# Two-layer graph network: both halves of eight weight chunks made inside the edge loop, one-hots for two edge tiles at once, biases by TensorE, second node half first

## The reference

```python
# layer 0
feat  = concat([x[src], x[dst]], axis=1)              # 8192 x 2048
e_f   = relu(feat @ W_kind + b_kind)                  # kind hh: 128 edges, oo: 640, ho: 7424
logit = e_f @ W_a + b_a
alpha = softmax of logit over the edges of one target
z     = segment_sum(alpha * x[src], dst)              # 256 x 1024
new   = relu(concat([x, z], 1) @ W_hn + b_hn)         # nodes 0 to 63
        relu(concat([x, z], 1) @ W_on + b_on)         # nodes 64 to 255
x1    = layernorm(x + new)
# layer 1
h  = x1 @ W
e  = exp(-leaky_relu((h @ a_l)[src] + (h @ a_r)[dst]))
hp = segment_sum(e * h[dst], src) / (rowsum + eps)
out = layernorm(x1 + elu(hp))
```

## Time and profile before

| | us |
|---|---|
| median of 3 runs | 383.04 (382.99 to 384.62) |
| the profiled execution | 383.35 |
| its span, first to last instruction | 381.3 |
| mean granted clock of TensorE | 0.934 of 2.4 GHz |
| TensorE (matmul) busy | 326.5 |
| VectorE busy | 301.9 |
| ScalarE busy | 189.9 |
| GpSimd busy | 136.8 |

### The profile page before, as it was taken

One profiled execution on the slowest core, in us unless ns is written; L12 is line 12 of the kernel. 1 busy time (PEld: TensorE's weight loads), 2 busy tenths in 40 slices (PEclk: granted clock), 3 DMA queues, 4 the chain that ended last, 5 costly groups with the idle time before them and its releaser, 6 DMA issues.

```text
span 381.3 us, 4671 instructions
## 1 busy us (share of the span) xinstructions
PE 326.5 (86%) x1434; PEld 252.7 (66%) x1434; DVE 301.9 (79%) x400; ACT 189.9 (50%) x289; POOL 136.8 (36%) x202
## 2 busy tenths in 40 slices
PE   2899999999999998999999999638899962898570
PEld 1678877776547866888888887426688841686320
DVE  0799999959799687999999997985677789436445
ACT  3745594220333349788787764250566581251143
POOL 3200070370008002988988773910024231016000
PEclk9999999999999999999999999885999995699685
DMA  7997698899989960002003003333638960000002
GB/s 232 412 400 292 238 345 298 278 244 275 354 297 377 388 243 2 0 3 112 0 2 111 3 3 89 131 110 119 211 106 332 306 250 2 0 2 1 0 0 110
DMA packets 17639, 63.63 MB, mean 167 GB/s; under 512 B 2234, under 2 KB 2236, under 8 KB 17360
## 3 DMA queue, kind: packets, MB, share of 16 engines
q1 hardware_dynamic: 13520, 50.34, 36.2%
q0 software_dynamic: 2096, 8.74, 7.8%
q10 hardware_dynamic: 2000, 4.26, 3.2%
HBM read 60.16 MB, written 3.16 MB: 166 GB/s over the span
## 4 chain that ended last, share of the span: by engine, by line
PE 64%; DVE 25%; DMA 4%; ACT 4%; issue 2%; SPq 0%; DVEq 0%; ACTq 0%
PE ps L1240 20%; PE ps L1067 10%; PE ps L1131 7%; DVE W_lo L669 6%; PE ps L1089 6%; PE ps L1247 3%; PE ps L1273 3%; PE ps L1106 3%; PE ps L1304 3%; PE ps L1336 3%; DMA W_raw<-in_L_gnn_W_dram 2%; PE ps L1281 2%; DMA x_nat<-in_x_dram 2%; DVE tile_val L690 1%; DVE small L957 1%
## 5 line engine op out<-in xcount | busy, mean ns | idle before, releaser
L432 ACT CAST W_hi<-W_raw 128x1024 fp32r<-128x1024 f32 x72 | 73.2, 1046 | 67.9 <-DMA W_raw<-in_L_gnn_W_ho_dram 24.6
L669 DVE TENSOR_TENSOR W_lo<-W_raw,W_hi 128x1024 fp32r<-128x1024 f32 x56 | 73.7, 1342 | 23.2 <-ACT W_hi L432 20.7
L905 DVE SCALAR_TENSOR_TENSOR ps<-ps,wa_bc 128x1024 f32<-128x1024 f32 x74 | 87.6, 1277 | 1.9 <-PE ps L1240 1.9
L364 POOL TENSOR_TENSOR W_lo<-W_raw,W_hi 128x1024 fp32r<-128x1024 f32 x16 | 39.4, 2468 | 82.0 <-ACT W_hi L432 82.0
L1240 PE MATMUL ps<-A_tab,oh 128*128 x148 | 53.5, 443 | 2.2 <-ACT oh L541 2.2
L390 POOL TENSOR_SCALAR sc_r<-irow,keys 128x64 f32<-128x64 f32 x74 | 35.0, 472 | 39.1 <-PE ps L1247 38.7
L1067 PE MATMUL ps<-W_hi,xT_hi 128*128 128x512 f32 x112 | 46.5, 415 | 0.9 <-DVE W_lo L669 0.9
L1240 PE MATMUL ps<-B_tab,oh 128*128 x148 | 46.4, 394 | 0.0
L1067 PE MATMUL ps<-W_lo,xT_hi 128*128 128x512 f32 x112 | 44.1, 394 | 0.0
L547 ACT ACTIVATE sc_l<-sc_l,keys 128x64 f32<-128x64 f32 x74 | 24.6, 341 | 21.8 <-DVE ps L905 15.5
L1067 PE MATMUL ps<-W_hi,xT_lo 128*128 128x512 f32 x112 | 34.5, 390 | 0.0
(11 more groups left out here) (229 smaller groups left out, 546.7 us busy)
## 6 DMA issues: line engine op xcount, KB each, us to landing
W_raw<-in_L_gnn_W_oo_dram SPq DMA_DIRECT2D x8, 1024.0 KB, 9.7
W_raw<-in_L_gnn_W_ho_dram SPq DMA_DIRECT2D x8, 1024.0 KB, 4.9
W_raw<-in_L_gnn_W_hh_dram SPq DMA_DIRECT2D x8, 1024.0 KB, 8.4
W_raw<-in_L_gnn_W_hn_dram SPq DMA_DIRECT2D x8, 1024.0 KB, 5.3
W_raw<-in_L_gnn_W_on_dram SPq DMA_DIRECT2D x8, 1024.0 KB, 6.0
W_raw<-in_L_gnn_W_dram SPq DMA_DIRECT2D x4, 1024.0 KB, 7.6
key_rows<-key_rows_scratch POOLq DMA_DIRECT2D x1, 2304.0 KB, 14.0
table_scratch<-tabs ACTq DMA_DIRECT2D x2, 1024.0 KB, 6.4
```

Source lines behind the costliest of these rows:

```text
L364: ga.tensor_tensor(W_lo[:, ring(n), :], W_raw[:, n // 2 % NS, n % 2, :], W_hi[:, ring(n), :].bitcast(F32), ALU.subtract).then_inc(lo_pool, 1)
L432: sa.copy(W_hi[:, ring(n), :], W_raw[:, n // 2 % NS, n % 2, :]).then_inc(hi_made, 1)
L669: v.tensor_tensor(W_lo[:, ring(n), :], W_raw[:, n // 2 % NS, n % 2, :], W_hi[:, ring(n), :].bitcast(F32), ALU.subtract).then_inc(lo_made, 1)
L905: v.scalar_tensor_tensor(acc, acc, 0.0, wa_bc[:], ALU.max, ALU.mult, accum_out=keys[:, t, 2:3]).then_inc(reduced, 1)
```

## The change

Six edits:

1. In the loop GpSimd makes the four one-hots of two tiles by two instructions over 256 elements (subtract, then compare with zero). They wait for the scatter of tile t-3. `sc_l` and `sc_r` become one buffer `sc`.
2. GpSimd makes the low halves of all eight chunks 48 to 55 in the loop (after tiles 8, 16, ..., 64), and ScalarE the eight high halves. Chunks 52 to 55 ("apart") have high halves in buffers of their own and low halves in place in `W_raw`. The transfers into these places wait until the chunks are used. From chunk 56 on GpSimd begins only after P.
3. The maximum of the static logits is taken ahead of the loop, so that behind it only the new part is reduced.
4. The biases `b_hn` and `b_on` are split into two parts and added by six matmuls of TensorE; VectorE's additions L976 and L982 go. ScalarE copies 64x2048 elements, VectorE subtracts 32x2048, GpSimd makes the pick matrix.
5. The update's order changes, so that the hn chunks end four chunks before the last; rows 0 to 63 are finished early.
6. The late half 1 of the nodes goes first through the layernorm and into layer 1. x1's half 0 is transposed between chunks 81 and 82 of half 1. The low halves of chunks 80 to 82 are made after the first part of half 0.

```diff
+        def apart(n):
+            return END["hoB"] + NB <= n < UX
+        def in_ring(n):
+            return [m for m in range(n + 1) if split(m) and not apart(m)]
+        def halves(n):
+            if apart(n):
+                return hi_apart[n - END["hoB"] - NB], lo_in_raw[:, n // 2 % NS, n % 2, :]
+            return W_hi[:, ring(n), :], W_lo[:, ring(n), :]
...
-        END = {"ooA": 8, "ooB": 16, "hoA": 30, "hh": 40, "hoB": 48, "updx": 64, "upd": 80, "h1": 88}
+        END = {"ooA": 8, "ooB": 16, "hoA": 30, "hh": 40, "hoB": 48, "hn": 76, "upd": 80, "h1": 88}
+        update_order = [("hn", 0), ("on", 0), ("hn", 2), ("on", 2), ("hn", 4), ("on", 4), ("hn", 6), ("hn", 8), ("on", 6),
+                        ("hn", 10), ("on", 8), ("hn", 12), ("on", 10), ("hn", 14), ("on", 12), ("on", 14)]
...
# SyncE
-                    if not split(last_of):
+                    if not split(last_of) or apart(last_of):
                         sp.wait_ge(chunk_used, last_of + 1)
...
# GpSimd, ends(t)
                 if t >= U:
-                    pool.wait_ge(scattered, 1 + JO + t - U + 1)
-                ga.tensor_scalar(sc_r[:, t % U, :], irow[:, 1:Q + 1], keys[:, t, 0:1], None, ALU.is_equal)
-                ga.tensor_scalar(sc_l[:, t % U, 1, :], irow[:, 1:Q + 1], keys[:, t, 1:2], None, ALU.is_equal) \
-                  .then_inc(ends_made, 1)
+                    pool.wait_ge(scattered, 1 + JO + t + 2 - U)
+                pair = sc[:, t % U:t % U + 2, 0:2, :]
+                link(ga.tensor_tensor(pair, irow[:, 1:Q + 1].unsqueeze(1).unsqueeze(1).broadcast_to([P, 2, 2, Q]),
+                                      keys[:, t:t + 2, 0:2].unsqueeze(3).broadcast_to([P, 2, 2, Q]), ALU.subtract))
+                ga.tensor_scalar(pair, pair, 0.0, None, ALU.is_equal).then_inc(ends_made, 1)
...
-            for t in range(NT):
+            for t in range(0, NT, 2):
                 ends(t)
-                if t % 12 == 8 and t // 12 < NB:
-                    lows(END["hoB"] + t // 12, END["hoB"] + t // 12 + 1)
-
-            lows(END["hoB"] + NB, len(chunks))
+                if t % 8 == 0 and 8 <= t <= 64:
+                    lows(END["hoB"] + t // 8 - 1, END["hoB"] + t // 8)
+
+            pool.wait_ge(gathered, NT)
+            link(ga.memset(pick_f[:], 0.0))
+            for r in (0, Q // 2):
+                link(ga.memset(pick_f[r:r + 1, 0:P], 1.0))
+            ga.nop().then_inc(pick_made, 1)
+            pool.wait_ge(dve_step, dve_at("P"))
+            lows(UX, len(chunks))
...
# ScalarE, in the loop
-                if j % 6 == 3 and j // 6 < NB:
-                    high(END["hoB"] + j // 6)
+                if j % 4 == 2 and END["hoB"] + j // 4 < UX:
+                    high(END["hoB"] + j // 4)
...
# ScalarE, behind the loop
-            highs(END["hoB"], END["hoB"] + NB)
+            act.wait_ge(pick_made, 1)
+            sa.copy(pick[:], pick_f[:])
+            act.wait_ge(biases_in, 112)
+            sa.copy(bn_parts[:], bn_rows).then_inc(act_step, 1)
+            high(UX)
+            high(UX + 1)
...
# VectorE
+            top = soft.rearrange("p (h n) -> p h n", h=2)
+            link(v.tensor_tensor(top, S_log[:, 0, :, :], S_log[:, 1, :, :], ALU.max))
+            link(v.tensor_reduce(small[:, 44:46], top, AX, ALU.max))
...
-            link(v.tensor_tensor(top_static[:], top_static[:], S_log[:, 2, :, :], ALU.max))
-            link(v.tensor_reduce(small[:, 2:4], top_static[:], AX, ALU.max))
+            link(v.tensor_reduce(small[:, 2:4], S_log[:, 2, :, :], AX, ALU.max))
+            link(v.tensor_tensor(small[:, 2:4], small[:, 2:4], small[:, 44:46], ALU.max))
...
             lows(UX, UX + NB)
+            dve.wait_ge(act_step, act_at("parts"))
+            link(v.tensor_tensor(bn_parts[Q // 2:Q], bn_rows[Q // 2:Q], bn_parts[Q // 2:Q].bitcast(F32), ALU.subtract))
+            stage("parts")
...
-            for q, acc in ((0, G0[:, D:2 * D]), (1, G1[:, 0:D])):
-                own = slice(q * Q, (q + 1) * Q)
-                dve.wait_ge(act_step, act_at(f"q{q}_low"))
-                link(v.tensor_tensor(y2[own, 0, :], y2[own, 0, :], bn_bc[own, 0, :], ALU.add))
-                link(v.tensor_tensor(y1[own, 0, :], y2[own, 0, :], acc[own, :], ALU.add))
-            link(v.scalar_tensor_tensor(y1[:, 0, :], y1[:, 0, :], 0.0, x_nat[:, 0, :], ALU.max, ALU.add))
+            dve.wait_ge(act_step, act_at("q0_low"))
+            link(v.tensor_tensor(G0[0:Q, D:2 * D], G0[0:Q, D:2 * D], y2[0:Q, 0, :], ALU.add))
+            link(v.scalar_tensor_tensor(y1[0:Q, 0, :], G0[0:Q, D:2 * D], 0.0, x_nat[0:Q, 0, :], ALU.max, ALU.add))
+            lows(END["upd"], END["upd"] + NB - 1)
+            dve.wait_ge(chunk_used, END["upd"])
+            link(v.scalar_tensor_tensor(y1[:, 1, :], G1[:, D:2 * D], 0.0, x_nat[:, 1, :], ALU.max, ALU.add))
+            statistics(1)
+            stage("var1")
+            dve.wait_ge(act_step, act_at("q1_low"))
+            link(v.tensor_tensor(G1[Q:P, 0:D], G1[Q:P, 0:D], y2[Q:P, 0, :], ALU.add))
+            normalise_second_half(x1[:, 1, :], "sd1")
+            stage("x1_1")
+            link(v.scalar_tensor_tensor(y1[Q:P, 0, :], G1[Q:P, 0:D], 0.0, x_nat[Q:P, 0, :], ALU.max, ALU.add))
             statistics(0)
             stage("var0")
...
+            x1_low(1)
+            first_half_scale("sd0")
+            stage("scale0")
+            lows(END["upd"] + NB - 1, END["upd"] + NB)
+            x1_low(0)
...
# TensorE, behind the second part of z
+                if s == 1:
+                    pe.wait_ge(dve_step, dve_at("parts"))
+                    for acc, k, columns in ((G0[:, D:2 * D], 0, slice(Q, Q + P)), (G1[:, 0:D], 1, slice(Q, Q + P)),
+                                            (G1[:, D:2 * D], 1, slice(0, P))):
+                        for f in range(0, D, 512):
+                            mm(acc[:, f:f + 512], pick[:, columns], bn_parts[:, k, f:f + 512], start=False, stop=False,
+                               skip_group_check=True)
...
+            transpose_x1(1)
             for g in range(END["upd"], END["h1"], NB):
-                block_by_block(g, G1, END["upd"], "x1T", "h_0" if g + NB == END["h1"] else None)
+                block_by_block(g, G1, END["upd"], "x1T", "h_1" if g + NB == END["h1"] else None, (1, 0),
+                               (lambda: transpose_x1(0)) if g == END["upd"] else None)
```

More of the change, by code:

```diff
@@ L429, in high @@
                 act.wait_ge(w_in[n // 2 % NS], 16 * (n // 2 // NS + 1))
-                if n >= NB:
-                    act.wait_ge(chunk_used, before_in_ring(n) + 1)
-                sa.copy(W_hi[:, ring(n), :], W_raw[:, n // 2 % NS, n % 2, :]).then_inc(hi_made, 1)
+                if len(in_ring(n)) > NB and not apart(n):
+                    act.wait_ge(chunk_used, in_ring(n)[-1 - NB] + 1)
+                sa.copy(halves(n)[0], W_raw[:, n // 2 % NS, n % 2, :]).then_inc(hi_made, 1)
             def highs(a, b):
@@ L580, in _ @@
                     .then_inc(act_step, 1)
[L581 removed]
+            high(UX + 2)
+            high(UX + 3)
             for s in range(2):
@@ L612, in normalise_first_half, with x1_high @@
                     .then_inc(act_step, 1)
+            def x1_high(h):
+                act.wait_ge(pe_step, pe_at(f"x1T{h}"))
+                sa.copy(xT_hi[:, :, h * P:(h + 1) * P], G0[:, h * D:(h + 1) * D].rearrange("p (c n) -> p c n", n=P)) \
+                    .then_inc(act_step, 1)
+            act.wait_ge(dve_step, dve_at("var1"))
+            deviation(1)
+            x1_high(1)
             act.wait_ge(dve_step, dve_at("var0"))
@@ L617, in _ @@
             normalise_first_half(x1[:, 0, :])
-            act.wait_ge(dve_step, dve_at("var1"))
-            deviation(1)
-            for h in range(2):
-                act.wait_ge(pe_step, pe_at(f"x1T{h}"))
-                sa.copy(xT_hi[:, :, h * P:(h + 1) * P], G0[:, h * D:(h + 1) * D].rearrange("p (c n) -> p c n", n=P)) \
-                    .then_inc(act_step, 1)
+            x1_high(0)
             highs(END["upd"], END["h1"])
             warm_up(ACT.Exp, 1)
-            for h in range(2):
+            for h in (1, 0):
                 act.wait_ge(dve_step, dve_at(f"dots{h}"))
@@ L668, in low @@
                     dve.wait_ge(hi_made, hi_count(n))
-                    v.tensor_tensor(W_lo[:, ring(n), :], W_raw[:, n // 2 % NS, n % 2, :],
-                                    W_hi[:, ring(n), :].bitcast(F32), ALU.subtract).then_inc(lo_made, 1)
+                    hi, lo = halves(n)
+                    v.tensor_tensor(lo, W_raw[:, n // 2 % NS, n % 2, :], hi.bitcast(F32), ALU.subtract).then_inc(lo_made, 1)
             def lows(a, b):
@@ L1056, in split_chunk @@
                 pe.wait_ge(lo_pool if by_pool(n) else lo_made, lo_count(n, by_pool(n)))
-                return W_hi[:, ring(n), :], W_lo[:, ring(n), :]
+                return halves(n)
             def dense(a, b, acc, hi, lo, blocks, first, end):
@@ L1075, in x_dense, with block_by_block @@
```

(12 more changed lines are left out.)

120 lines of the change are left out of this document (61 added, 59 removed).

## The result

| | before | after |
|---|---|---|
| median (lowest to highest) | 383.31 (382.99 to 384.62), 4 runs | 377.38 (376.57 to 378.31), 4 runs |
| profiled execution, its span | 383.35, 381.3 | 376.57, 374.5 |
| mean granted clock, of 2.4 GHz | 0.934 | 0.950 |

After over before is 0.984 (95% interval 0.981 to 0.987): 1.6% faster, 5.9 us at the medians. 372.0 was forecast and the range ended at 377.0. The kernel is faster, as said, but gives half of the gain; the time is just outside the range. The profiled execution was the fastest of the four, so the traces show 6.8 us of gain and the medians 5.9.

What follows compares the result with a forecast made beforehand. VectorE was taken to pace the loop and softmax, TensorE the update, VectorE's work the standstill before layer 1. Terms -8.2 - 0.9 + 1.4 - 7.3 + 1.5 + 2.5 = -11.0 from 383.35 gave 372.3, 372.0 as median; range 368 to 377.

Steps and rivals of the forecast that it cites:

- What bounds the kernel: Whole kernel: loop at VectorE's pace with TensorE close behind, softmax VectorE's, update TensorE's, then TensorE stands still before layer 1.
- 8.45 us transfer: Before layer 1: low halves of chunks 80 and 81 waited 8.45 us for a transfer, ahead of VectorE's node halves.
- Softmax: Behind the loop: without GpSimd beside them VectorE's operations run short and the merged maximum saves a pass; 8.2 us less.
- P to z: From P to z's low half: TensorE's clock stays up or falls late, VectorE's bias subtraction caps the gain; 0.9 less.
- Biases on TensorE: In the update: six added matmuls of 512 columns cost 1.4 us more.
- Tail: From the update's last matmul to layer 1: half 1 goes first, low halves 80 to 82 lie ahead; 7.3 us less.
- Layer 1: In layer 1: half 0's transposes between chunks 81 and 82 add 1.0 to 2.0 us, taken as 1.5.
- The loop: Edge loop: each of eight low halves between pairs holds TensorE by 0.7 us, of which 2.5 us more is left.
- the dearer loop: Edge loop: pair near 1.9 us or ScalarE late with eight high halves; +3 to +6, 375 to 378; chance 0.10.
- The slower case: Edge loop: GpSimd becomes the loop's engine through costly rows of 64; 385 at a pair of 2.5 us; chance 0.06.
- free loop: Edge loop costs nothing because the compare runs faster than the 2048-element row; 369.5 us (368 to 371); chance 0.26.
- The page on one-input operations: GpSimd in the loop: page says one-input operations run roughly at line-rate; pair near 1.3 us, loop would cost nothing.

Runs made afterwards that it cites:

- e7: Kernel before, with VectorE's low halves of chunks 80 and 81 moved from ahead of the first layernorm to behind x1; 385.3 us, 1.005 of before.
- e5: Changed kernel with GpSimd's low halves of chunks 52 to 55 behind the loop again, the other four in the loop; 378.1 us, 0.987 of before.
- e2: Changed kernel with end one-hots made for one tile at a time again, all eight low halves still in the loop; 370.8 us, 0.966 of before.
- e6: Kernel before with only the paired end one-hots, four buffers, four low halves in the loop; 385.9 us, 1.008 of before.
- e8: e1 plus 14 extra matmuls keeping TensorE busy until about P, and VectorE's bias subtraction moved behind z's first part; 369.1 us, 0.964 of before.
- e1: Changed kernel with six buffers for the end one-hots instead of four; 371.0 us, 0.967 of before.
- e9: e1 plus only the 14 extra matmuls on TensorE, results unused; 373.3 us, 0.973 of before.

## Why the prediction was wrong, step by step

- **What bounds the kernel: right**, except for the 8.45 us transfer, which I read as something the tail stood behind and which holds nothing (e7).
- **Softmax: right**, -8.2, with the four durations as forecast. e5 shows the price of contention depends on which instructions meet, which I needed only for before.
- **P to z: the size agrees, -1.1 for -0.9, but partly by luck.** The forecast had the clock stay up or fall late. It fell as before, and rose about 3.7 us behind the start of the first 16 matmuls in place of 6.0 (estimates from the windows of both traces). Kernels with the same code there took 8.8 to 9.3 (e2 to e5), and those with the old code 8.6 (e6) and 9.6 (e7), so a term of 1.1 is no larger than what this stretch varies by itself. That VectorE's bias parts cap the gain was right in kind: with both causes gone there are 2.3 more (e8).
- **Biases on TensorE: right.** The six matmuls take 1.58 us in the chain; forecast 1.4.

```profile
258.61 5.55 PE ps L1357 x16
...
267.25 3.72 PE ps L1357 x16
...
275.57 1.58 PE ps L1366 x6
```

- **Tail: right**, -6.8 for -7.3; it is 10.2 in every kernel with the change and 16.9 to 17.0 in the kernel before and e6. The low halves of chunks 80 to 82 end at 310.47, 0.4 behind TensorE's last matmul, which is most of what is missing; the prediction had named this risk. **Layer 1: +1.2 for +1.5**, also partly by luck: half 0's transposes take 0.87, below the 1.0 to 2.0 forecast, and the kernels with the old order take 23.5 (before), 24.0 (e7) and 24.6 (e6).
- **The loop: wrong, and it is the step that failed.** The mechanism was named (a pair, a low half and the next pair stand ahead of a scatter), but its price was not: +2.5 was forecast, +6.5 measured, and 96.0 is over the 92 that the prediction gave as a sign of being wrong. Its sum was 8 x 0.7 for the stalls, less 1.3 of head start, less 1.8 that TensorE regains. The stall itself was nearly right: I put 0.7, from 6.3 for GpSimd's path and 5.6 for TensorE's; measured are 5.95 (1.55 + 2.37 + 1.53 + 0.5) and 5.36, so about 0.58. A cheaper pair and a faster TensorE cancel. The term that failed is the one that I put at nothing: **TensorE pays 0.48 to restart behind a scatter that waited**, so a stall is 1.06 and eight are 8.5 for 5.6, 2.9 more. The other 1.1 is in what I took off. The head start was worth 0.7 and not 1.3 (at the first stall, 1.06, the spacing of VectorE's reductions grew by 0.35), and it is never rebuilt. The regain is 1.06 - 0.88 = 0.18 between two low halves, 1.3 over seven intervals and not 1.8 over the loop. So all seven later stalls came through: 7 x 0.88 + 0.3 = 6.5, the measured term. I also let the loop go free at a pair of 1.54. By that formula the measured pair of 1.53 would have cost nothing, and the kernel would have come to 369.5; the path of TensorE in it, 5.6 for 5.36, was too long.
- **Of the rivals** the dearer loop (375 to 378) is what happened, though by neither cause it named: the pair was not near 1.9 and ScalarE was not late (it waits 19.8 us for GpSimd). It had 0.10. The slower case did not come, but its direction did in e6: the pairs alone make the old kernel slower. That the chances were 0.26 for a free loop and 0.10 for a dear one was wrong: I took the uncertainty to lie in the pair's duration alone, and held the allowance of four tiles as exact.
- **The page on one-input operations:** the compare takes 0.85 for 256 elements. With the fixed part of 0.32 that is 2.1 ns per element, near the 2.49 I read from the earlier trace rows, where VectorE's own one-input operation took 0.42 for 512, 0.8 ns per element. The Trainium skill, GPSIMD Engine Reference, Engine selection ("roughly line-rate") is not borne out here. It would have been the wrong question either way.

## What to carry to other kernels

These are lessons of one kernel. On an engine that feeds others through a ring of buffers, count latency, not load: the longest instruction that can stand ahead of a small one, plus everything bound to the same wait, must fit into the ring's depth. Putting two small operations into one instruction makes the ring shallower; do it only with more buffers, or cut the long instruction. Count, too, what the waiting engine needs to go on. And where two causes end within a microsecond of each other, test them together as well as alone: here one alone gave a loss, the other nothing in its own stretch, both gave 1.9 there. Before a difference of a microsecond is put down to an edit, look at the granted clock of the stretch: here it moved the loop by 0.7 between e1 and e9 and layer 1 by 1.3 between e1 and e8, with the same code in these stretches.
